# Experts' combination: GpSimd in place of VectorE adds the scaled rows of the second rank

## The reference, cut to what matters

```
probs = softmax(x @ gate_w.T);  w, idx = top_k(probs, 2);  w = w / sum(w)
out[t] = w[t,0] * expert[idx[t,0]](x[t]) + w[t,1] * expert[idx[t,1]](x[t])     (layer 2: plus a shared expert)
x = x + 0.5 * out
```

## Time and profile before

| | us |
|---|---|
| timed runs: median of 3 (lowest to highest) | 3646.06 (3645.56 to 3650.42) |
| profiled execution: span from first to last instruction | 3752.3 |
| profiled execution: time of its own outside the span | not shown |
| busy in the span: PE / DVE / ACT / POOL | 3149.9 / 2516.1 / 1992.9 / 1210.8 |
| one combination, first weighted add to last sum | 17.7 to 19.0 |

### The profile page before, as it was taken

One profiled execution on the slowest core, in us unless ns is written; L12 is line 12 of the kernel. 1 busy time (PEld: TensorE's weight loads), 2 busy tenths in 40 slices (PEclk: granted clock), 3 DMA queues, 4 the chain that ended last, 5 costly groups with the idle time before them and its releaser, 6 DMA issues. The chain is left out here.

```text
span 3752.3 us, 61710 instructions
## 1 busy us (share of the span) xinstructions
PE 3149.9 (84%) x20415; PEld 1980.8 (53%) x20415; DVE 2516.1 (67%) x6929; ACT 1992.9 (53%) x2981; POOL 1210.8 (32%) x1282
## 2 busy tenths in 40 slices
PE   4669999786659967999999599687778885998899
PEld 2533333344448842222222488566666674887687
DVE  8888997675974468999995744543585345666565
ACT  1238988663214446999999144322332234664564
POOL 3454550112456631101010566366434651001000
PEclk8879999997859988999999699799898897999899
DMA  1043430000021132000000411401201113000100
GB/s 55 1 130 124 131 126 13 1 1 23 1 115 42 43 103 61 27 20 28 20 20 2 168 42 43 140 29 44 75 24 61 43 40 113 1 1 1 65 9 12
DMA packets 87167, 187.18 MB, mean 50 GB/s; under 512 B 23168, under 2 KB 41408, under 8 KB 83792
## 3 DMA queue, kind: packets, MB, share of 16 engines
q1 hardware_dynamic: 60048, 117.66, 9.3%
q0 software_dynamic: 26816, 65.58, 5.7%
HBM read 121.23 MB, written 61.34 MB: 49 GB/s over the span
## 5 line engine op out<-in xcount | busy, mean ns | idle before, releaser
L2486 ACT ACTIVATE core_pr<-core_two 128x1024 f32<-128x1024 f32 (+3 forms) x896 | 787.6, 935 | 49.3 <-PE core_two L2453 45.5
L2522 DVE TENSOR_REDUCE core_mx<-core_one 128x1 f32<-128x512 f32 x778 | 491.8, 685 | 20.9 <-PE core_one L2405 13.6
L2465 PE MATMUL core_ps_o<-core_pr,core_vals 128*32 128x512 f32 (+3 forms) x3584 | 434.5, 560 | 1.8 <-ACT core_oT L2497 1.5
L2405 PE MATMUL core_one<-arena,queries 64*128 64x512 bf16 (+3 forms) x1472 | 375.5, 363 | 29.8 <-PEq L62 19.6
L2453 PE MATMUL core_two<-queries,arena 64*128 64x512 bf16 (+3 forms) x1792 | 341.5, 360 | 9.4 <-ACT core_pr L2486 6.8
L2405 PEld LDWEIGHTS core_one<-arena,queries 64*128 64x128 bf16 x1472 | 113.3, 94 | 297.7 <-DVE core_mx L2522 132.4
L2339 POOL COPY core_vals<-arena 128x288 f32<-128x288 f32 x32 | 14.7, 459 | 692.1 <-PE core_ps_o L2465 692.1
L2516 DVE CUSTOM_DVE_ANT_0 core_junk<-core_one,core_over 128x512 bf16<-128x512 f32 (+4 forms) x334 | 201.9, 644 | 26.2 <-PE core_one L2405 21.4
L2453 PEld LDWEIGHTS core_two<-queries,arena 64*128 64x128 bf16 x1792 | 94.3, 94 | 201.7 <-ACT core_pr L2486 145.7
L2492 ACT ACTIVATE core_over<-core_two 128x1024 f32<-128x1024 f32 (+4 forms) x167 | 159.9, 958 | 58.4 <-PE core_two L2428 45.3
L424 POOL DMA_INDIRECT expert_out<-arena,moe_second_dest_index x142 | 139.9, 985 | 149.9 <-ACT arena L600 129.9
(11 more groups left out here) (614 smaller groups left out, 8184.0 us busy)
## 6 DMA issues: line engine op xcount, KB each, us to landing
arena<-expert_out SPq DMA_DIRECT2D x64, 256.0 KB, 3.8
expert_rows<-arena SPq DMA_DIRECT2D x13, 512.0 KB, 12.5
core_w_raw<-in_m_up POOLq DMA_DIRECT2D x25, 256.0 KB, 3.4
m_hi<-core_w_hi POOLq DMA_DIRECT2D x25, 256.0 KB, 2.4
m_lo<-core_w_lo POOLq DMA_DIRECT2D x25, 256.0 KB, 3.0
q_parts<-qkv_parts SPq DMA_DIRECT2D x16, 384.0 KB, 2.6
k_parts<-qkv_parts SPq DMA_DIRECT2D x16, 384.0 KB, 3.4
queries<-q_parts SPq DMA_DIRECT2D x64, 96.0 KB
```

The lines of the kernel that those rows point to most:

```text
L2405: pe.matmul(one[bank[e]][:, 0:width], q_sb[rows, hq, pair, qt * P:(qt + 1) * P], k_sb[rows, hq, pair, kc * CW:kc * CW + width], start=True ...
L2465: mm = pe.matmul(ps_o[h * 32:(h + 1) * 32, off:CW], vals[:, hq % 2, j, h, :], pr[:, (n * N2 + k) % KEPT, h // 2, h % 2, off:CW], start=(j ...
L2486: a.activation(pr[:, step % KEPT, i, :, off:CW], two[spot[e] % 2][:, :, off:CW], ACT.Exp, scale=HD ** -0.5).then_inc(s_wide, 1)
L2522: v.tensor_reduce(at, scores, AX.X, ALU.max).then_inc(s_read, 1)
```

## The change

DVE no longer adds the second rank; POOL does, with an instruction of the same kind, shape and operands, behind its scatters. POOL's `power` for the next stage moves behind its add of chunk 4. DVE's list keeps its eight groups of weighted adds, the statistics and the normalising. What ACT, SP and PE do is the same, and so is what each load waits for: `s_sum`, which POOL raises now.

```
@@ block.gpsimd, after the last scatter
-            if head:
-                head.power(p)
+            for c in range(CHUNKS):
+                p.wait_ge(s_pair, c + 1)
+                p.wait_ge(s_scaled, c + 1)
+                xc = tile_of(g.x, c * CT, CT)
+                p.tensor_tensor(xc, xc, both[:, c % 4, 1], ALU.add).then_inc(s_sum, 1)
+                if c == AT and head:
+                    head.power(p)
@@ block.vector
-            for c in range(CHUNKS + 1):
-                if c < CHUNKS:
-                    v.wait_ge(s_yl[c % 4], 16 * TOPK * (c // 4 + 1))
-                    weighted(c, 0).then_inc(s_pair, 1)
-                if c:
-                    v.wait_ge(s_pair, c)
-                    v.wait_ge(s_scaled, c)
-                    xc = tile_of(g.x, (c - 1) * CT, CT)
-                    v.tensor_tensor(xc, xc, both[:, (c - 1) % 4, 1], ALU.add).then_inc(s_sum, 1)
+            for c in range(CHUNKS):
+                v.wait_ge(s_yl[c % 4], 16 * TOPK * (c // 4 + 1))
+                weighted(c, 0).then_inc(s_pair, 1)
                 if c == AT and head:
                     v.wait_ge(s_sum, 2)
                     head.statistics(v)
```

## The result

| | before | after |
|---|---|---|
| median of 6 timed runs (lowest to highest), us | 3645.81 (3639.94 to 3650.42) | 3671.31 (3663.51 to 3677.38) |
| ratio after / before, with its 95% interval | | 1.0068 (1.0056 to 1.0080) |

The change makes the kernel slower by 25.5 us. The profiled execution of the kernel after spans 3670.4 us and took 3672.25 us by its own time.

A forecast was written before the change was run, and what follows sets the result against it. PE is busiest overall, but the change lies in four combinations where PE idles and DVE's sums or POOL's drain end last. 5.3 us of later POOL ends plus 20.0 of tails: 3646.1 + 25.3 = 3671 us, range 3665 to 3678.

The forecast's parts named there:

- The stretches pass everything on: Four experts' combinations before a barrier, PE idle: whatever such a stretch gains or loses reaches the kernel's time whole.
- The cycle of 2.1 us: Per chunk in the combinations: POOL's add 1.27, blocked weighted adds 0.67, handover 0.15; 2.1 us against 1.66 before.
- POOL's last add ends 16.6 us behind chunk 1, 18.7 in moe1_second: Summed steps from chunk 1's arrival to add 7's end; moe1_second longer because it treats 8 tiles.
- Hindering: In the combinations, POOL's adds and DVE's weighted adds and normalising block each other for whole instructions, some DVE ones taking 1.2 to 1.5.
- Rival A: Drain tail follows POOL's last add, but POOL and DVE don't hinder each other: +10, 3656 us; chance 0.09.
- Statistics free: DVE's one-input statistics run unhindered beside POOL's adds; if blocked too, 1.2 us a stage more.
- The load pause: Pause in the loads between chunks 3 and 4 closes as the first sum comes earlier; loads don't enter the sum.
- C: Rival: faster, as chunk 4's load starts 2.3 us earlier and each stage ends with POOL's add: -10, 3636; chance 0.06.
- The tails: POOL's drain before the barrier outlasts its last instruction by 3.7 us (layer 1) or 6.3 (layer 2); now uncovered, 20.0 in all.
- POOL's later end: POOL's adds end later than the four stages' ends before, 5.3 us of the total.
- The sum a stage: Added time per experts' stage, POOL's later end plus tail: 5.7, 5.7, 6.9 and 7.0 us.
- Rival B: POOL and DVE hinder each other, but the drain's tail doesn't move: +5.3, 3651 us; chance 0.13.

The follow-up runs named there:

- the memset kernel: Kernel after with each POOL add replaced by a memset about as long that reads nothing, second-rank sum left out: 3660.34 us, ratio 1.0052.
- the drain moved ahead: Kernel after with an explicit POOL drain behind the last scatter, ahead of POOL's adds: 3650.82 us, ratio 1.0022.
- the second profile of before: Kernel before, unchanged, run once more for another profile: 3641.28 us; the profile spans 3639.5 us, its four stretches 63.5 us together.
- a tiny instruction: Kernel before plus a one-column memset on POOL behind DVE's last sum in each experts' stage: 3668.50 us, ratio 1.0066.

## Why the prediction was right

Forecast 3671, measured 3671.31. That the two agree to 0.3 us is luck, since the timed difference itself is known to 4 us or so; what can be judged is the steps. Each against its rows:

- **The stretches pass everything on.** Right: +24.6 in the four stretches, +25.5 in the time; the other stages are the same within a few us of either sign.
- **The cycle of 2.1 us.** 2.06. A cycle without blocking would have been 1.3. POOL's adds take 1.25 to 1.31, one 1.40.
- **POOL's last add ends 16.6 us behind chunk 1, 18.7 in moe1_second.** 16.3, 18.8, 16.4 and 16.5. In moe1_first the parts are: add 4 ended at +8.95 (8.9 by the terms), `power` at +10.3 (10.2), add 5 at +11.5 (11.5), add 6 at +13.3 (13.5), add 7 at +16.3 (16.6). Here and in both stages of layer 2, within 0.3, the terms are right one by one, not only in the sum. In moe1_second two errors cancel: add 5 begins 12.3 behind chunk 1 instead of 11.2, since POOL waits 0.97 for the statistics of eight tiles, and the 0.7 that add 6 was to wait for chunk 6's weighted adds does not arise.
- **Hindering.** Right: five of the TENSOR_SCALARs took 1.28 to 1.30, each beside an add. That it works by whole instructions and only against a POOL instruction that reads, in the case of the weighted adds, the memset showed. Rival A had no hindering and +10; the memset kernel, which keeps only the part of the normalising, has +14.4.
- **Statistics free.** Right: all 20 of the four stages take 0.27 to 0.28 in the kernel after, with an add beside some of them.
- **The load pause.** Half right. The pause behind chunk 3 closed, but a shorter one came ahead of chunk 5, whose load now waits for POOL's second add. In moe1_first (window, length, busy times, clock, DMA share, GB/s):

```profile
1341.00:1342.00 1.00, 0.00 (x0) 0.00 (x0) 1.00 (x5) 0.98 (x4) 0.37 (x1) 0.50 0.18 41
```

DVE is busy all through it and waits for no load from chunk 3 on, so the loads had no part in the time, as said for this change. What the prediction did not see, and rivals A and C leaned on, is that DVE hardly waited for the load behind the pause in the kernel before (0.4 to 0.5 us over the four stages); the kernel in which POOL adds chunk 0 only showed it.
- **The tails.** The heart of the prediction. 5.0 and 7.6 were forecast, 4.97, 4.98, 7.59 and 7.57 came. Four uncovered tails were put at 20.0 us; taking them away gave 19.7.
- **POOL's later end.** 5.3 forecast, 4.8 with the drain moved ahead.
- **The sum a stage.** 5.7, 5.7, 6.9 and 7.0 forecast; from chunk 1 on, 5.1, 5.6, 6.9 and 6.9 against the second profile of before.
- **The sum by the page's figure.** The figure of the Trainium skill (GPSIMD Engine Reference, "Elementwise — side-by-side cycle accounting"), 4497 ns for 2048 values and so 1.1 us by the estimate of a quarter, was said to lower the sum by some 3 us. With 1.1 instead of 1.27 for seven adds a stage it is 4.8 (an estimate too). Nothing rests on it, and the adds took 1.25 to 1.31.
- **The basis.** Taking the 25 over whole from an execution 2.9% longer was right, because what was longer in it lay for the most part in the slots (103 of 113 us between the two profiles of before) and not in the combinations (63.4 and 63.5).

Rival B's number, 3651, is where the kernel after lands once a drain stands behind the last scatter: 3650.82. The rival described the kernel that one added instruction makes of it.

Shown are thus the tail (by a tiny instruction, and by taking it away), its independence of what POOL does last, and that the weighted adds' share of the blocking is worth 9 to 10 us. Only argued is the share of the normalising, which was not run by itself.

## What to carry to other kernels

Before work is put on an engine that looks idle, look at what its list ends with: work behind POOL's indirect DMAs moves a drain of several us from a covered place to the path, whatever the work is. If POOL must work behind them, put a drain straight behind the last DMA, where POOL waits anyway. And count an add moved from DVE to POOL at the sum of both engines' time when both read two SBUF tiles, as in the cycle of 2.06 us here, not at the longer of the two.

## What the runs showed that was not expected

- The length of POOL's drain follows the number of places of the gathers' ring: a tail of 3.7 us with 8, 6.3 with 24, and 3.7 again in layer 2 with 8.
- A drain with indirect DMAs still under way took 9.1 to 17.8 us, and it lengthened the next one in layer 1 (3.9 to 5.35) and shortened it in layer 2 (6.5 to 4.0).
- The tail isn't peculiar to the experts' stages. One other stage has DMAs on POOL, an attention with 108 direct ones, and its drain takes 9.16 us, 8.9 of them behind POOL's last instruction; in the eleven stages without DMAs on POOL the drain ends within 0.1 us of it. Its row in the kernel after:

```profile
L62 POOLq DRAIN  x1: 9156/9156/9156, 632.3 to 632.3; - x1
```

- One memset of one column a stage, where POOL would have had nothing to do, cost 24.3 us of 3644 by the median (interval 18 to 30), 18.7 by the stretches.
- The same kernel takes 3644 us on one chip and 3749 on another, and most of the difference lies in the slots with POOL's indirect DMAs (19 to 33 us a stage); the combinations don't differ.
